# A decoder layer on one core: feed-forward tiles in other PSUM banks, and three steps that change places in the queues

## The reference

```
x1  = ln(x + attention(x))                 # 16 heads of 32, softmax, low-rank additions to q, k, v, o
x2  = ln(x1 + x1 * scan(ctx * ctx))        # r = decay * r + ctx^2 along the 256 rows
h   = gelu(silu(act_quant(rms_norm(x2)) @ ternary(w1).T + b1))        # 2048 wide
z   = layer_norm(h) * ln_g + ln_b
out = ln(x2 + act_quant(rms_norm(z)) @ ternary(w2).T + b2)
```

## Time and profile before

| | us |
|---|---|
| median of 3 runs | 1042.36 |
| the profiled execution | 1039.61 |
| its span, first to last instruction | 1037.8 |
| mean granted TensorE clock | 0.966 |
| PE busy | 941.8 (91% of the span) |
| DVE busy | 859.1 (83%) |
| ACT busy | 826.3 (80%) |
| POOL busy | 548.5 (53%) |

### The profile page before, as it was taken

One profiled execution on the slowest core, in us unless ns is written; L12 is line 12 of the kernel. 1 busy time (PEld: TensorE's weight loads), 2 busy tenths in 40 slices (PEclk: granted clock), 3 DMA queues, 4 the chain that ended last, 5 costly groups with the idle time before them and its releaser, 6 DMA issues.

```text
span 1037.8 us, 23337 instructions
## 1 busy us (share of the span) xinstructions
PE 941.8 (91%) x9244; PEld 647.8 (62%) x9260; DVE 859.1 (83%) x1490; ACT 826.3 (80%) x957; POOL 548.5 (53%) x767
## 2 busy tenths in 40 slices
PE   5998987999999999999999999999999999977515
PEld 3766756676777667676767767676767777654102
DVE  4578868889797989889897979898897979897766
ACT  3646686888989798888888897988889897977684
POOL 2332338274654639373755647383746546472643
PEclk9999998999999999999999999999999999999768
DMA  9432200313132222323141212323131412122213
GB/s 361 158 113 113 73 3 21 75 49 88 22 85 52 55 62 56 81 53 85 27 110 22 75 46 61 71 53 85 52 85 22 97 40 75 22 63 54 53 34 89
DMA packets 106351, 73.67 MB, mean 71 GB/s; under 512 B 91385, under 2 KB 91385, under 8 KB 104450
## 3 DMA queue, kind: packets, MB, share of 16 engines
q1 hardware_dynamic: 105522, 70.34, 25.3%
q10 hardware_dynamic: 720, 1.84, 0.5%
HBM read 41.73 MB, written 8.40 MB: 48 GB/s over the span
## 4 chain that ended last, share of the span: by engine, by line
DVE 33%; PE 25%; ACT 17%; issue 13%; POOL 7%; DMA 3%; SPq 1%; DVEq 0%; ACTq 0%; POOLq 0%
PE bank L1484 8%; PE bank L1345 7%; DVE neg_max L965 6%; POOL h L549 5%; DVE stats L1022 3%; ACT h L727 3%; DVE h L1096 3%; ACT junk L737 3%; ACT h L742 3%; DVE fz L1101 2%; DVE qk_parts L988 2%; PE bank L1485 2%; ACT L727 2%; DVE rows L1038 2%; DVE qx L1063 2%
## 5 line engine op out<-in xcount | busy, mean ns | idle before, releaser
L965 DVE TENSOR_REDUCE neg_max<-wave 128x8 f32<-128x2048 f32 x64 | 146.2, 2284 | 29.4 <-PE wave L1370 29.4
L549 POOL TENSOR_TENSOR h<-h,g_tile 128x2048 f32<-128x2048 f32 x30 | 139.2, 4640 | 39.1 <-ACT h L742 39.1
L659 ACT ACTIVATE probs<-wave 128x1024 f32<-128x1024 f32 x128 | 124.2, 1023 | 28.2 <-PE wave L1394 27.9
L1484 PE MATMUL bank<-w,xqT 128*128 128x512 fp8e4 x496 | 130.0, 385 | 17.5 <-DMA xqT<-xq 13.6
L439 POOL TENSOR_SCALAR attn_hi<-attn 128x256 fp32r<-128x256 f32 x64 | 28.3, 442 | 174.3 <-DVE attn L1004 159.4
L697 ACT ACTIVATE rows<-rows,rstd 128x512 f32<-128x512 f32 x96 | 74.4, 807 | 41.9 <-POOL rstd L455 23.7
L1096 DVE TENSOR_TENSOR h<-h,b_tile 128x2048 f32<-128x2048 f32 x32 | 84.1, 2629 | 18.6 <-POOL h L549 18.0
L721 ACT ACTIVATE h<-bank,qx 128x512 f32<-128x512 f32 x124 | 82.3, 689 | 20.0 <-PE bank L1485 16.7
L1491 PE MATMUL bank<-w,hqT 128*128 128x512 fp8e4 x416 | 94.3, 380 | 0.3 <-DMA hqT<-h 0.3
L1484 PEld LDWEIGHTS bank<-w,xqT 128*128 128x128 bf16 x496 | 46.7, 99 | 74.9 <-DMA xqT<-xq 9.9
L1345 PE MATMUL bank<-xT_hi,wq_hi 128*128 128x256 f32 x256 | 78.8, 308 | 0.1
(11 more groups left out here) (184 smaller groups left out, 2736.9 us busy)
## 6 DMA issues: line engine op xcount, KB each, us to landing
ctx_sb<-ctxT SPq DMA_DIRECT2D x16, 512.0 KB, 3.7
rows<-x SPq DMA_DIRECT2D x16, 512.0 KB, 4.0
out<-rows SPq DMA_DIRECT2D x32, 256.0 KB, 2.1
xT_in<-xT SPq DMA_DIRECT2D x15, 512.0 KB, 4.0
h<-w1T SPq DMA_DIRECT2D x4, 1024.0 KB, 14.0
h<-w2T SPq DMA_DIRECT2D x4, 1024.0 KB, 5.0
h<-Wq SPq DMA_DIRECT2D x1, 1024.0 KB, 5.9
h<-Wk SPq DMA_DIRECT2D x1, 1024.0 KB, 9.4
```

The lines of the kernel that those rows point to most:

```text
L549: po.tensor_tensor(h_of(b, q)[:, :], h_of(b, q)[:, :], g_tile[:, :], ALU.mult).then_inc(done, 1)
L659: ac.activation(probs[:, kt, :, :], wave[:, :, kt * T:(kt + 1) * T], ACT.Exp, scale=SM_SCALE).then_inc(S["probs_ready"], 1)
L965: dv.tensor_reduce(neg_max[:, :, :], wave[:, :, :].rearrange("p j (t k) -> p j t k", t=NT), axis=AX_X, op=ALU.max, negate=True).then_inc(S ...
L1484: pe.matmul(p[:, :], xqT[:, q, kc, :], w1[:, kc, n * FW:(n + 1) * FW], start=(kc == 0), stop=False)
```

## The change

Five things change, and no arithmetic with them. (1) `f(3)` to `f(7)` get the banks 6, 1, 2, 3, 7 in the place of 6, 7, 4, 6, 7: three of the tiles now lie in `wave`. (2) `shifted(j, 0)`, which writes all four banks of `wave`, moves from the end of one PE body to behind `y(j, 0)` at the start of the next, and waits for the seventh silu; `weighted(., 0)` waits for the third silu in place of the sixth, since bank 4 now only holds `f(2)`. (3) On DVE `quantise_z(0)` goes ahead of `z_add(1)`. (4) On ACT `z_square(1)` goes from ahead of `zq_store(0)` to a place between the fourth and the fifth silu. (5) On DVE `scan` goes ahead of `quantise_z(1)`, and POOL's `res2` waits for the end of that rounding in place of the scan's.

```
         bank_no = {u[:2]: 6 + i % 2 for i, u in enumerate(users)}
-        bank_no.update({("f", u): (6, 7, 4)[u % 3] for u in range(8)})
+        bank_no.update({("f", u): (6, 7, 4, 6, 1, 2, 3, 7)[u] for u in range(8)})
...
                     neg_mean(j - 2, 0)
-                    wait(po, "scan_done", j - 1, 5)
+                    if alive(j, 3):
+                        wait(po, "z_quant", j - 3, 12)
+                    else:
+                        wait(po, "scan_done", j - 1, 5)
                     res2(j - 2)
...
                     ctx_square(j)
                 if alive(j, 2):
-                    z_square(j - 2, 1)
                     zq_store(j - 2, 0)
...
                     shiftT(j + 1, 0)
+                if alive(j, 2):
+                    z_square(j - 2, 1)
                 if alive(j, 1):
                     silu(j - 1, 1)
...
                 if alive(j, 2):
+                    quantise_z(j - 2, 0)
                     z_add(j - 2, 1)
-                    quantise_z(j - 2, 0)
...
                     qk_lo(j + 1, 1)
+                if alive(j, 0):
+                    scan(j)
                 if alive(j, 2):
                     quantise_z(j - 2, 1)
-                if alive(j, 0):
-                    scan(j)
...
                 wait(pe, "shiftT_stored", b, c + 1)
+                if c == 0:
+                    wait(pe, "silu_done", b - 2, 7)
...
                 if c == 0 and b >= 2:
-                    wait(pe, "silu_done", b - 2, 6)
+                    wait(pe, "silu_done", b - 2, 3)
...
                     y(j, 0)
+                shifted(j, 0)
...
                         f(j, u)
-                if alive(j, -1):
-                    shifted(j + 1, 0)
```

More of the change, by code:

```diff
@@ L1605, in lead @@
                 shiftT(1, 0)
-                shifted(1, 0)
             def body(j):
```

## The result

| | before | after |
|---|---|---|
| median of 17 runs each, us | 1042.87 (1039.0 to 1045.04) | 1045.57 (1042.2 to 1048.37) |
| the profiled execution, us (span) | 1039.61 (1037.8) | 1045.57 (1043.8) |
| granted clock, mean over the span | 0.966 | 0.958 |
| first `f` of body 2 to that of body 14, us | 689.15 | 693.88 |
| PE busy / DVE busy / ACT busy, us | 941.8 / 859.1 / 826.3 | 944.2 / 877.1 / 820.0 |

The changed kernel takes 1.0030 times as long, with a 95% interval of 1.0017 to 1.0043: slower by 0.3%, which is 1.8 to 4.5 us. The forecast was 1046.1 us.

What follows compares the result with a forecast made beforehand. PE, the fullest engine, was held by a loop through the last silu and the second r; +3.5 (loop) + 0.3 (late xq) + 0.35 (body 14) - 0.4 (drain) = +3.7, giving 1046.1 us, range 1036.5 to 1050.

Steps and rivals of the forecast that it cites:

- The loop: First f, last silu, 26.63 to the second r, 20.58 to the next first f: 57.72 against 57.43, +3.5 over twelve.
- The square behind `shiftT`: On ACT, z_square(1) before the fifth silu moves the gelu's table load from +9.76 to +10.51 after the first f.
- The wait at `f(3)`: On PE, f(3) waits 0.38 for the silu that empties bank 6; claimed to go, -0.38 per usual body.
- Late transposes: Transposed xq landing late (5.4 in place of 3.4): the delay now stays in the loop, +0.3 in all.
- Body 14: Later gelu's table load in front of a last body that waits for DVE and the DMA: +0.35.
- The drain: Last body, without qk_hi or shiftT between the silu: the square fits, the f(3) wait goes, -0.4.
- Costed at nothing: Hidden edits (shifted behind y, scan and res2 order, spread banks), put at 0, bounds -0.1 to +0.3 per body.
- the bound of the rival: Upper bound for hidden edits: res1 on POOL beside DVE's rounding holds up the ln3 sum, +0.3 per body.
- A: Faster: the last silu isn't on the loop, bodies take 56.97, 1036.5 us in all; chance 0.22.
- B: About the same: half of the square's visible 0.75 is found again, loop 57.35, 1041.5 us; chance 0.15.
- the 0.75: Part of the 1.89 us square on ACT that shows as delay of the last silu; 1.14 lies in gaps.
- C: Much slower: the longer wait at the second r brings PE to half clock, 1050 to 1058 us; chance 0.07.

Runs made afterwards that it cites:

- sq_half: Changed kernel with z_square(1) over only 1024 of 2048 columns for batches 0 to 13, so its result is not the layer's; 1038.50 us (1 run).
- sq_more: Changed kernel with a second, unused square of 512 columns right ahead of z_square(1) for batches 0 to 13; 1052.28 us (1 run).
- sq_early: Changed kernel with z_square(1) moved on ACT to between the second and third silu; 1038.42 us (8 runs), 0.9966 times the kernel before.
- ln3_early: sq_early with DVE's second ln3 sum moved ahead of qk_lo(3), its statistics left behind; 1043.68 us (12 runs), 1.0022 times the kernel before.
- scan_last: Changed kernel with scan behind the last rounding again and res2 waiting for the scan as before; 1050.11 us (1 run).

## Why the prediction was right, and where its sizes were off

The mechanism came as told: the square behind `shiftT` delays the last silu and with it the loop. The sizes of the loop fit to 0.07 for a body. The parts beside the loop did not, and part of the agreement of the total is luck.

- **The loop.** First `f`, last silu, gelu's table load, second `r`, next first `f`: the prediction had 26.63 and 20.58 unchanged, and they are (26.62 and 20.59 in the table). sq_half, sq_more and sq_early move its first part alone and the body follows each time.
- **The square behind `shiftT`.** Forecast +6.08 for its start, +7.97 for the fifth silu, +9.80 for the last, +10.51 for the gelu's table load. Measured from 597.01: +6.09, +7.99, +9.70, +10.44. The last 0.07 is in the silu, which come every (606.71 - 605.00) / 3 = 0.57 where the earlier trace rows gave 0.61.
- **The body.** 57.72 forecast, 57.65 measured. The wait at `f(3)` went, as forecast, and the one at `r` grew: its weight load waited 0.6 before and 1.1 after; 0.5 and 1.2 were forecast.
- **Late transposes.** Forecast +0.3 in all. Twelve bodies of 57.65 make 691.80, and 693.88 were taken: 2.1 more. Of these, 1.7 lie in bodies 7, 10 and 13, whose last part, from the second `r` to the next first `f`, is 1.0, 0.4 and 0.2 longer than 20.6; after body 7 the next first `f` waits 0.86 for xq, as shown above, and after body 10 0.24. Against 57.36 before, whose twelve make 688.32, that sum was 0.8. So lateness costs 1.3 more and not 0.3. About 0.7 of it is what the prediction named, a delay that is no longer paid back: before, the gelu's table load came at +9.83 in body 3 and +9.76 in body 8 in place of +10.16; after, it comes at +10.43 in body 8 too. The other 0.6 is that more of it was late in this execution (landings of up to 5.9, before 5.4), and whether the change has a part in that is open. The direction was right, the size a quarter.
- **A base that was mixed.** The sum set a body free of lateness, 57.72, against the mean of before, 57.43, which has the 0.8 in it; the same body of before is 57.36. So the 0.3, as it was added, stood for the whole 2.1.
- **Body 14** +0.41, forecast +0.35.
- **The drain, the part that failed.** Forecast -0.4; measured +0.99 in body 15 and +0.50 behind it. The order of body 15 does what was said (no square in the way, no wait at `f(3)`). But the clock was costed for the steady state alone, and here it counts. PE of the changed kernel, and behind it that of before:

```profile
941.66 1.86 PE L1490 MATMUL bank<-w,xqT 128*128 128x512 fp8e4 x4 [1.52 <-DMA xqT<-xq]
...
945.84 1.03 PE L1490 MATMUL bank<-w,xqT 128*128 128x512 fp8e4 x4
...
968.01 6.12 PE L1521 MATMUL wave<-w,hqT 128*128 128x512 fp8e4 x16 [4.63 <-DMA hqT<-h]
```

```profile
937.15 1.87 PE L1484 MATMUL bank<-w,xqT 128*128 128x512 fp8e4 x4 [3.56 <-DMA xqT<-xq]
...
940.69 1.03 PE L1484 MATMUL bank<-w,xqT 128*128 128x512 fp8e4 x4
...
963.31 5.31 PE L1515 MATMUL wave<-w,hqT 128*128 128x512 fp8e4 x16 [4.61 <-DMA hqT<-h]
```

  The first two of the eight `f` take 4.18 now and took 3.54: the granted clock is 0.50 from 942 to 944 and 0.55 from 944 to 946, where before it was 0.51 from 938 to 940 and 1.00 from 940 to 942. That eats up the wait at `f(3)`, and the gelu's table load of body 15 comes +11.57 behind its first `f`, before +11.38. The last `y` of the body takes 6.12 in place of 5.31 for the same 16 products, at a granted clock of 0.50 from 968 to 972 where before it was 0.50 from 964 to 966 and 0.68 from 966 to 968, and this 0.8 is the rest of the 0.99. Across the twelve kernels the load comes at +9.95 to +12.49, and not in the order of their code: sq_half, with the shorter square, has +12.47 and sq_early +9.95, because its first three `f` take 6.16 and those of sq_early 3.65. The 0.50 behind body 15 was not traced. By itself this part would have raised the forecast by 1.9.
- **Why the total came out anyway.** Against the profiled executions the body was forecast 0.07 too long (0.84 over twelve), lateness, as it was added, 1.78 too short, the ends 1.89, body 14 0.06, and the lead, put at nothing, was 0.64 shorter: 3.7 - 0.84 + 1.78 + 1.89 + 0.06 - 0.64 = 5.95, and 6.0 were measured. For the medians, over 17 runs each, the difference is 2.7, so there the 3.7 was 1.0 too much. The point of 1046.1 stands 0.5 from the median because the median of before, too, came out 0.5 above the one of 3 runs that the forecast was added to. That is luck. The profiled execution of before was one of the fast ones of its scatter, that of after was at the median.
- **Costed at nothing.** `shifted` behind `y` and the scan's exchange were put at 0 and do cost nothing in the changed kernel, and the bound of the rival (POOL's `res1` beside DVE's rounding) didn't come. What the runs add is that undoing them costs 0.23 (`shifted`) and 0.32 (the scan) of a body, as undoing the banks costs 0.35: they were not neutral but needed, as covers for what the square makes late. The prediction said this of the banks and missed it for the other two.
- **The rivals.** A is refuted: the last silu has no slack in the order that was made. Its bodies of 56.97 are those of sq_early (56.99), since to hide the square is the same as to absorb it. B: nothing of the 0.75 was found again but 0.07; its own sum, 1042.36 - 1.0, gives 1041.4 and not 1041.5. C: the loop's clock stayed 1.00 in after (a wait of 1.1) and in sq_more (1.5).
- **What the working took too simply.** It gave the 0.5 at `r` to the chain from the gelu alone. ln3_early shows that most of it stays when the chain is early: the end of `y(1)`, DVE's sum and `r`'s start. In before, `r` waited 0.36, and 0.33 a body later, against the 0.19 that is left in ln3_early: the chain led this second bound by less than 0.2. The change lengthened the chain, so it didn't matter to the sum; to whoever would shorten the chain it is the next wall.

## What to carry to other kernels

Where an engine's instruction can be put anywhere in a stretch, put it ahead of instructions that would wait anyway: the same 1.9 us square cost 0.66 of a body after the fourth silu and nothing after the second, because behind the second the next silu would have waited for PE anyway, and behind the fourth no silu waits any more. To find whether an engine at 79% is on the path, look for a loop whose parts repeat to a hundredth from body to body, and shorten one of its parts by a known amount. And judge a package of edits by both halves, since what is worth nothing alone can be what makes the other half bearable.

## What the runs showed of the hardware

**Small DVE instructions beside POOL's sums.** In the changed kernel `quantise_z(1)`'s small steps on DVE fall together with POOL's `res1`. DVE and then POOL, changed kernel:

```profile
607.08 1.00 DVE L1123 TENSOR_TENSOR fz<-fz 128x1 f32<-128x1 f32 x1
```

```profile
606.52 2.76 POOL L498 TENSOR_TENSOR rows<-rows,bo_tile 128x512 f32<-128x512 f32 x2
```

The same L1123 took 0.16 in the same kernel where POOL was quiet:

```profile
591.98 0.16 DVE L1123 TENSOR_TENSOR fz<-fz 128x1 f32<-128x1 f32 x1
```

and over the whole kernel its mean rose from 185 to 557 ns (30 each). L1126, which also reads two tiles, took 0.80 beside the same POOL sums; the steps between them with one input, L1124 and L1125, kept their 0.15 and 0.16. POOL is slowed likewise: its 128x1 step L487 took 1.54 in scan_last, beside a `TENSOR_TENSOR` of 1.21 on DVE, and 0.56 in the changed kernel. The Trainium skill (SBUF — State Buffer, Who interferes with whom) tells of a port pair that VectorE and GpSimd share and that either holds alone, so that certain instructions of the one block the other's. The trace agrees, with 0.16 against 1.00. The two steps alone grew by 19.6 us over the kernel, more than the 18.0 by which DVE's busy time did. Nothing followed: the body's 0.29 is accounted for by the square.

**A transpose that lands late.** The transposes of xq land after 3.4 us, or after up to 5.9. In the changed kernel, the DMA queues in the 3.5 us around a late one (533.3) and around a punctual one (592.0), each with its landing (queue and kind, packets, MB, share of the 16 engines):

```profile
q1 hardware_dynamic: 1316, 0.38, 82.5%
q14 instruction: 1, 0.01, 3.3%
q8 instruction: 1, 0.02, 1.7%
...
DMA to landing us min/median/max: 5.9/5.9/5.9
```

```profile
q1 hardware_dynamic: 1366, 0.44, 64.6%
...
DMA to landing us min/median/max: 3.4/3.4/3.4
```

Over the twelve kernels, 156 transposes: 58 had no transfer of the kind "instruction" near them and landed in 3.3 to 3.4 every time; 98 had one, and averaged 4.2, from 3.3 to 5.9. It is a coincidence in time, in every kernel at the same bodies; whether the fetch holds the transpose up was not tested.

**Waits of PE and its clock.** In the loop, a wait of 1.1 (after) or 1.5 (sq_more) in a body left the granted clock at 1.00; a wait of 2.13 was followed by 0.50. But the length of one wait doesn't decide it alone: in the same execution of before, a wait of 2.14 that ended at 931.66 was followed by no fall, and the granted clock was 1.00 in all windows from 930 to 936.
